# A fixed tile per expert for its last rows, and eight dense groups ahead of the expert stage

## The chip, the core and the metric

The kernel runs on one core of a Trainium2 chip, all in fp32. The metric is the device time of one execution in microseconds; times here are the median of three runs, and the profile is of one execution.

## What is computed

For x of 16 x 512 tokens of width 256, with xn = layernorm(x), the output is x + attn(xn) + ffn(xn):

```python
# attn: a diagonal state space model, then a gated FFN (D_FF = 688)
u = rmsnorm(xn, ssm_norm_w);  Bu = u @ B_w.T                  # 64 states
h_t = sigmoid(log_lambda) * h_(t-1) + Bu_t                    # along 512 tokens
x1 = xn + h @ C_w.T + D_skip * u;  z = rmsnorm(x1, ffn_norm_w)
attn = x1 + (silu(z @ w1.T) * (z @ w3.T)) @ w2.T
# ffn: 32 experts of inner width 128, 8 per token, and one shared expert (256)
scores = sigmoid(xn @ gate_w.T)       # top 8 within the 4 best groups of 4, normalised, times 2.5
ffn = sum_e combine[t, e] * (silu(xn @ w_gate[e].T) * (xn @ w_up[e].T)) @ w_down[e].T + shared(xn)
```

## The kernel before

The 8192 tokens are 64 tiles of 128 and 16 groups of four tiles (a group is one sequence of 512). Each of five engines runs its own instruction list, ordered by hand; semaphores tie them together.

**Stages.** First (a0) all groups are loaded, normalised and sent through the router. Then come the early dense groups 0 to 8 (FIRST = 9), then the expert stage, then the late dense groups 9 to 15.

**A dense group** (`pe_group`, `act_group`, `dve_group`) has eight steps s. Step s computes a gate and an up product (line 1263; steps 0 and 1 are the shared expert and read xT, the others read zT), ScalarE applies silu (648), VectorE multiplies (`h_tile`, 991), and TensorE adds the down product of the step before (1280). Between the steps stands the preparation of the next group: transposing its xn (step 1), B product (2), scan (3), C product and x1 (4), norm (5, 6), transposing z at the end. `finish_part` adds what the group gives to x + x1; SP stores early groups' sums in DRAM (`parts`).

**Routing** is VectorE's work, done in halves of 32 tiles within the early groups: choice of experts in groups 0 and 1 to 3, slots and bases at the end of groups 0 and 3 (`r_slots`, `r_bases`, 823 to 852), the slot table and the weights between steps 0 and 1 of groups 1 and 4 (`r_slot_table`, `r_weights`, 857 to 875), the experts of the tiles one step later (`r_tile_experts`).

**Slots.** In each half the rows of tokens are sorted by expert in DRAM (`sorted_rows`), 288 tiles of 128 rows for 256 tiles' worth of rows. An expert with n rows has ceil(n / 128) tiles. Those that form pairs come first, so that the first SAME = 128 of 144 pairs hold one expert; each odd last tile goes behind. Rows of a last tile that no token fills must be zero: tiles from 224 on are zeroed at fixed addresses, and one further 128-row store of zeros per expert goes to an address that `r_bases` computes (`pad_starts`): for half 0, 16 by SP and 16 by GpSimd (537), for half 1, 32 by SP (407). Then GpSimd scatters rows with their routing weights, one indirect DMA per tile and choice, 256 per half (546).

**Expert stage.** 288 pairs of tiles. Per pair: load rows, transpose (1336), gate and up products (`e_gu`, 1348: four matmul calls over 256 columns for one expert, eight over 128 for two; the trace has two matmuls per call), silu (680), product (1108), down product (1362), scaling (690, 1117), store to `results`. VectorE copies each pair's gate and up weights to a fixed place (1100): one block for one expert, two for two. Expert weights (`wexp`, 12.6 MB) lie in `big`, where the routing scratch, the x buffers (from AT_X) and the rows of half 0 (from AT_ROWS) were before; so SP loads them in parts as each gets free, the last ones behind the scatter of half 0 (420). GpSimd gathers each token's eight results (557), for half 0 within the pairs of half 1, for half 1 in the late stage; VectorE sums them (1009, 1016): half 0's within the pairs of half 1, half 1's (`combine`) in the late groups, four tiles in each, and the last four at the very end.

**Borders.** Into the experts: VectorE and ScalarE wait until all early sums are stored, TensorE for row loads and weights. Out of them, group 9 is prepared by itself:

```python
            transpose_x(FIRST)          # TensorE, after e_down(ALL - 1)
            bu_product(FIRST)
            bu_transpose(FIRST)
            y_product(FIRST)
            transpose_z(FIRST)
```

## Time and profile before

| | |
|---|---|
| median of three runs | 1827.65 us (1825.58 to 1830.5) |
| the profiled execution | 1828.46 us, its span 1826.8 us |
| granted TensorE clock, mean | 0.969 of 2.4 GHz |
| TensorE / VectorE / ScalarE / GpSimd busy | 1732.0 / 986.1 / 653.4 / 1042.6 us |
| early groups from, expert stage, late groups from | 88.6, 556.7 to 1459.9, 1489.3 us |

Times in rows are us from the span's start, unless they are called ns. PE is TensorE, PEld its weight loads, DVE VectorE, ACT ScalarE, POOL GpSimd, SP the engine that issues most DMAs. In a timeline "x8" stands for eight instructions put together, and the bracket is the idle time before them and what ended it. The clock column is the granted share of 2.4 GHz.

### The profile page before, as it was taken

Reading aid. Unit: us, or ns where it says so; the run is one execution under the profiler, and the core shown is the slowest. Engines: PE = TensorE matmul, PEld = TensorE weight load, DVE = VectorE, ACT = ScalarE, POOL = GpSimd, SP = SyncE. Lnnn points to the kernel's source line nnn. Section 1 sums busy time; section 2 is a strip of 40 time slices with the busy share of each in tenths; the row PEclk is TensorE's granted clock in tenths of the full one; section 3 lists DMA queues with packets and bytes.
Section 4 is the critical chain, followed back from the end, with each engine's and each line's share of the span. In section 5 each row is a group of like instructions: output and inputs, shape, how many; then the busy total and the mean of one; then the engine's idle time right before and its main releaser. Section 6 shows DMA issues by size and latency. Waiting matters only on the chain.

```text
span 1826.8 us, 26818 instructions
## 1 busy us (share of the span) xinstructions
PE 1732.0 (95%) x7846; PEld 1259.9 (69%) x7848; DVE 986.1 (54%) x2832; ACT 653.4 (36%) x1349; POOL 1042.6 (57%) x1058
## 2 busy tenths in 40 slices
PE   7797899899998999999999999999999969999996
PEld 3464565566666888888889888888888846666663
DVE  7487646633313444444445566666666535555555
ACT  6520221222213444444444444444444422222220
POOL 0002777777777777773000566666656077777773
PEclk9798999899998999999999999999999969999998
DMA  5964333636378999997555899999899554443332
GB/s 171 323 224 139 134 140 115 223 128 252 126 277 274 297 292 300 293 296 248 180 176 179 255 295 274 287 276 288 275 284 277 175 158 123 123 121 110 110 110 75
DMA packets 270790, 383.71 MB, mean 210 GB/s; under 512 B 30916, under 2 KB 235832, under 8 KB 269880
## 3 DMA queue, kind: packets, MB, share of 16 engines
q1 hardware_dynamic: 220584, 236.94, 41.1%
q0 software_dynamic: 49920, 145.03, 24.1%
q8 instruction: 66, 1.08, 0.2%
q14 instruction: 76, 0.62, 0.1%
q10 hardware_dynamic: 144, 0.03, 0.0%
HBM read 189.47 MB, written 192.42 MB: 209 GB/s over the span
## 4 chain that ended last, share of the span: by engine, by line
PE 89%; DVE 7%; issue 1%; ACT 1%; DMA 1%; DVEq 0%; SPq 0%; ACTq 0%
PE ps L1348 29%; PE ps L1263 19%; PE ps L1362 14%; PE ps L1280 11%; PE ps L1336 7%; PE ps L1183 2%; PE ps L1245 2%; PE ps L1216 2%; PE ps L1255 1%; PE ps L1232 1%; PE ps L1176 1%; DVE big L1009 1%; DMA big<-in_x 0%; PE ps L1239 0%; DVE arena L991 0%
## 5 line engine op out<-in xcount | busy, mean ns | idle before, releaser
L557 POOL DMA_INDIRECT xe<-results,slots x384 | 391.9, 1020 | 395.8 <-DMA results<-arena 217.4
L1348 PE MATMUL ps<-arena 128*128 128x256 f32 (+1 forms) x2560 | 573.5, 369 | 1.5 <-ACT arena L675 1.5
L1348 PEld LDWEIGHTS ps<-arena 128*128 128x128 f32 x2560 | 428.6, 190 | 106.1 <-ACT arena L675 66.0
L1100 DVE COPY arena<-big 128x512 f32 x320 | 138.7, 442 | 345.4 <-PE ps L1348 318.6
L546 POOL DMA_INDIRECT sorted_rows<-big,slots x256 | 260.5, 1017 | 84.0 <-issue 77.8
L1362 PE MATMUL ps<-big,arena 128*128 x1152 | 296.4, 380 | 0.3 <-DVE arena L1108 0.3
L546 POOL DMA_INDIRECT sorted_rows<-xe,slots x256 | 248.3, 970 | 78.1 <-issue 78.1
L1263 PE MATMUL ps<-arena,w 128*128 128x512 f32 x640 | 288.4, 593 | 0.0
L648 ACT ACTIVATE arena<-ps 128x512 f32<-128x512 f32 (+1 forms) x128 | 76.4, 597 | 559.4 <-PE ps L1263 515.5
L991 DVE TENSOR_TENSOR arena<-arena,ps 128x512 f32<-128x512 f32 (+1 forms) x128 | 88.0, 688 | 329.3 <-ACT arena L648 328.2
L680 ACT ACTIVATE arena<-ps 128x256 f32<-128x256 f32 x288 | 110.6, 384 | 377.0 <-PE ps L1348 377.0
L1362 PEld LDWEIGHTS ps<-big,arena 128*128 128x128 f32 x1152 | 196.4, 190 | 15.4 <-issue 0.7
L1263 PEld LDWEIGHTS ps<-arena,w 128*128 128x128 f32 x640 | 122.2, 191 | 119.5 <-issue 115.2
L1280 PE MATMUL ps<-w,arena 128*128 128x256 f32 (+1 forms) x768 | 186.3, 385 | 1.7 <-DVE arena L991 1.7
L675 ACT ACTIVATE arena<-ps 128x512 f32<-128x512 f32 x288 | 172.1, 597 | 26.1 <-PE ps L1336 11.0
L1336 PE MATMUL ps<-ident,arena 128*128 128x128 f32 x1152 | 173.8, 274 | 6.4 <-DMA arena<-sorted_rows 6.4
L1280 PEld LDWEIGHTS ps<-w,arena 128*128 128x128 f32 (+1 forms) x768 | 142.8, 191 | 50.7 <-issue 31.1
L1117 DVE TENSOR_SCALAR arena<-ps,wcol 128x256 f32<-128x256 f32 x288 | 139.0, 483 | 68.1 <-PE ps L1362 60.4
L690 ACT ACTIVATE arena<-ps,wcol 128x256 f32<-128x256 f32 x288 | 136.6, 474 | 92.6 <-PE ps L1362 91.0
L1336 PEld LDWEIGHTS ps<-ident,arena 128*128 128x128 f32 x1152 | 143.5, 141 | 32.8 <-issue 6.9
L557 POOL DMA_INDIRECT big<-results,slots x128 | 130.4, 1019 | 39.0 <-issue 39.0
L1263 PE MATMUL ps<-arena,shgu 128*128 128x512 f32 x256 | 123.4, 638 | 7.1 <-DVEq L819 7.1
(186 smaller groups left out, 1402.8 us busy)
## 6 DMA issues: line engine op xcount, KB each, us to landing
arena<-sorted_rows SPq DMA_DIRECT2D x288, 288.0 KB
results<-arena SPq DMA_DIRECT2D x288, 256.0 KB, 3.6
sorted_rows<-big SPq DMA_DIRECT2D x2, 9216.0 KB, 47.3
big<-in_x SPq DMA_DIRECT2D x32, 512.0 KB, 4.5
sorted_rows<-big SPq DMA_DIRECT2D x48, 144.0 KB, 1.9
xe<-results,slots POOLq DMA_INDIRECT x384, 4.0
out<-xe SPq DMA_DIRECT2D x48, 128.0 KB, 3.9
big<-in_wexp SPq DMA_DIRECT2D x1, 5632.0 KB, 19.3
```

Source lines behind the costliest of these rows:

```text
L546: pool.indirect_dma_start(out=sorted_rows[half], out_offset=bass.IndirectOffsetOnAxis(ap=slots[:, half * HT + t, k:k + 1], axis=0), in_=ro ...
L557: pool.indirect_dma_start(out=gathered_at[place(i)][:, k, :], out_offset=None, in_=results[half], in_offset=bass.IndirectOffsetOnAxis(ap=s ...
L675: nc.scalar.activation(rT[n % 2], ps[:, n % 2, :], ACT.Copy).then_inc(rT_ready, 1)
L680: nc.scalar.activation(eg[n % 2], ps[:, 2 + n % 2, 0:2 * P].rearrange("p (s i) -> p s i", s=2), ACT.Silu).then_inc(eg_ready, 1)
L690: nc.scalar.activation(ey[n % RING][:, 0, :], ps[:, 4 + 2 * (n % 2), 0:D], ACT.Copy, scale=wcol[:, n % RING, 0:1]).then_inc(ey_act, 1)
L1100: last = nc.vector.tensor_copy(wgu[n % 2][:, s, :], big[:, ds(at_w, 4 * INNER)])
L1117: tsc(ey[n % RING][:, 1, :], ps[:, 5 + 2 * (n % 2), 0:D], wcol[:, n % RING, 1:2], None, ALU.mult).then_inc(ey_dve, 1)
L1263: last = mm(ps[:, 2 + 2 * (s % 2) + u, :], w[:, u, c, lo:lo + P], src[:, c, :], start=c == 0, stop=c == DC - 1)
L1280: last = mm(ps[:, 6 + t // 2, (t % 2) * D:(t % 2 + 1) * D], h[c % HR][at_p, t * P:(t + 1) * P], w, start=False, stop=s == CH - 1 and t % 2 ...
L1336: last = tp(ps[:, n % 2, j * P:(j + 1) * P], rows[n % RING][:, s, c * P:(c + 1) * P], ident[:, :])
L1348: last = mm(ps[:, 2 + n % 2, (2 * u + s) * P:(2 * u + end) * P], wgu[n % 2][:, s, at_w:at_w + INNER], rT[n % 2][:, (2 * c + s) * P:(2 * c ...
L1362: last = mm(ps[:, 4 + 2 * (n % 2) + s, 0:D], eh[n % 2][:, s, :], big[:, ds(at_w + 2 * D, D)], start=True, stop=True)
```

## The change

An expert with n rows now has floor(n / 128) full tiles, in pairs first as before and then singly, and always one more tile, number 256 + e of the half, for the rest. Tiles from 224 on are zeroed at fixed addresses as before; all of `store_padding` goes, on SP and on GpSimd. The full tiles can fill fewer pairs surely: SAME is 96 in place of 128. The sorted rows have 288 tiles in each half as before, and so the stage 288 pairs.

FIRST is 8. Group 8 is still prepared within group 7, but its products come first of the late stage. Its xT, zT and its sum x + x1 are kept in DRAM meanwhile and loaded again near the end of the expert stage. The scatter is counted in eighths, and the weights over the rows of half 0 are loaded in eight parts.

```diff
-    SAME = HT * K // 2
-    USED = 2 * SAME - E
-    SPAN = NSLOT + E * P
+    FULL_TILES = HT * K
+    SAME = FULL_TILES // 2 - E
+    USED = FULL_TILES - E
+    SPAN = NSLOT
...
-    FIRST = 9
+    FIRST = HT // GT
     LATE = range(FIRST, GROUPS)
-    QUARTER = HT // 4
+    PIECES = 8
+    PIECE = HT // PIECES
...
-            def store_padding(half, es):
-                sp.wait_ge(starts_ready, half + 1)
-                sp.wait_ge(padded[half], 16)
-                for e in es:
-                    start = sp.value_load(pad_starts[half][0:1, e:e + 1], min_val=0, max_val=SPAN - P)
-                    sp.dma_start(sorted_rows[half][ds(start, P), :], pad_row).then_inc(padded[half], 16)
...
-            store_padding(0, range(E // 2))
             for g in range(FIRST - 1):
-                if g + 4 < FIRST:
+                if g + 4 <= FIRST:
...
-            sp.wait_ge(x_used, FIRST)
-            load_wexp(AT_X, AT_ROWS)
-            sp.wait_ge(xposed, FIRST)
-            for j in range(4):
-                sp.wait_ge(scattered[0][j], 16 * K * QUARTER)
-                load_wexp(AT_ROWS + j * QUARTER * ROW, AT_ROWS + (j + 1) * QUARTER * ROW)
-            store_part(FIRST - 1)
...
-            sp.wait_ge(zposed, FIRST)
-            sp.wait_ge(gu_ready, CH * (FIRST - 1) + 2)
-            sp.wait_ge(rms_z_ready, FIRST)
+            def load_wexp_over_rows(j):
+
+                sp.wait_ge(scattered[0][j], 16 * K * PIECE)
+                load_wexp(AT_ROWS + j * PIECE * ROW, AT_ROWS + (j + 1) * PIECE * ROW)
+
+            sp.wait_ge(x_used, FIRST)
+            sp.wait_ge(xposed, FIRST)
+            for j in range(PIECES - 1):
+                load_wexp_over_rows(j)
+            sp.wait_ge(xT_ready, FIRST + 1)
+            sp.dma_start(kept_xT, xT.rearrange("p c n -> p (c n)")).then_inc(xT_stored, 16)
+            sp.wait_ge(x_used, FIRST + 1)
+            load_wexp(AT_X, AT_ROWS)
+            sp.dma_start(group_rows(parts, FIRST), part_early[FIRST % 2]).then_inc(part_kept, 16)
+            sp.wait_ge(xT_stored, 16)
+            sp.wait_ge(y_ready, FIRST + 1)
+            sp.wait_ge(z_ready, FIRST + 1)
+            scattered_all(sp, 0)
             for n in range(RING):
                 load_rows(n)
+            load_wexp_over_rows(PIECES - 1)
+            sp.wait_ge(zT_ready, FIRST + 1)
+            sp.dma_start(kept_zT, zT.rearrange("p c n -> p (c n)")).then_inc(zT_stored, 16)
+            store_part(FIRST - 1)
...
+                    if m == ALL - 3:
+                        sp.dma_start(xT.rearrange("p c n -> p (c n)"), kept_xT).then_inc(xT_reloaded, 16)
...
-            sp.wait_ge(wgu_ready, ALL)
-            for g in range(FIRST, FIRST + 4):
+            for q in range(2):
+                sp.wait_ge(ey_stored[q], 16 * (ALL // RING))
+            sp.wait_ge(zT_stored, 16)
+            sp.dma_start(zT.rearrange("p c n -> p (c n)"), kept_zT).then_inc(zT_reloaded, 16)
+            for g in range(FIRST + 1, FIRST + 5):
                 load_x(g, g)
-            for i in range(HT, HT + GT):
-                load_part(i)
+            sp.wait_ge(part_kept, 16)
+            sp.dma_start(part_of(FIRST), group_rows(parts, FIRST)).then_inc(part_reloaded, 16)
             for g in LATE:
                 for t in range(GT):
-                    store_out((g - 1) * GT + t)
-                    if t == 2 and g + 4 < GROUPS:
-                        sp.wait_ge(x_used, g + 1)
-                        load_x(g + 4, g + 4)
+                    if g > FIRST:
+                        store_out((g - 1) * GT + t)
+                    if t == 2 and g + 5 < GROUPS:
+                        sp.wait_ge(x_used, g + 2)
+                        load_x(g + 5, g + 5)
...
-            pool.wait_ge(starts_ready, 1)
-            pool.wait_ge(padded[0], 16)
-            for e in range(E // 2, E):
-                start = pool.value_load(pad_starts[0][0:1, e:e + 1], min_val=0, max_val=SPAN - P)
-                pool.dma_start(sorted_rows[0][ds(start, P), :], pad_row).then_inc(padded_by_pool, 16)
-            pool.wait_ge(padded_by_pool, 16 * (E // 2))
-            pool.wait_ge(padded[0], 16 * (E // 2 + 1))
             for half in range(HALVES):
-                if half:
-                    pool.wait_ge(padded[1], 16 * (E + 1))
+                pool.wait_ge(padded[half], 16)
...
-            act.wait_ge(ey_dve, ALL)
-            xT_copy(FIRST)
-            results_stored(act, ALL)
-            rms_z(FIRST)
-            zT_copy(FIRST)
...
-            def r_bases(half):
-
-                tsc(nt_u, ne, float(P - 1), None, ALU.add)
+            def r_bases():
+
                 do(nc.vector.tensor_copy(full_u, ne))
-                tsc(nt_u, nt_u, P.bit_length() - 1, None, ALU.logical_shift_right)
                 do(tsc(full_u, full_u, P.bit_length() - 1, None, ALU.logical_shift_right))
                 nc.vector.memset(ones_e, 1.0)
-                nc.vector.tensor_copy(unused_f, unused_u)
+                nc.vector.tensor_copy(part_at, part_u)
                 nc.vector.tensor_copy(full, full_u)
-                tsc(two_u, nt_u, 1, None, ALU.logical_shift_right)
-                do(nc.vector.tensor_copy(ntf, nt_u))
+                do(tsc(two_u, full_u, 1, None, ALU.logical_shift_right))
                 do(nc.vector.tensor_copy(two, two_u))
-                tt(in_part, ntf, full, ALU.subtract)
                 do(tsc(two, two, 2.0, None, ALU.mult))
-                tt(odd, ntf, two, ALU.subtract)
+                tt(odd, full, two, ALU.subtract)
+                tsc(cut_part, full, float(P), None, ALU.mult)
                 do(nc.vector.tensor_tensor_scan(endt, ones_e, two, 0.0, ALU.mult, ALU.add))
                 do(nc.vector.tensor_tensor_scan(end_odd, ones_e, odd, 0.0, ALU.mult, ALU.add))
-                tsc(first_odd, endt[:, E - 1:E], float(2 * SAME), None, ALU.max)
                 tt(base, endt, two, ALU.subtract)
-                do(tsc(cut, two, float(P), None, ALU.mult))
+                tsc(cut, two, float(P), None, ALU.mult)
                 do(tsc(end_odd, end_odd, first_odd, None, ALU.add))
+                tt(apart_part, part_at, end_odd, ALU.subtract)
                 do(tt(apart, end_odd, odd, ALU.subtract))
-                tt(full, full, base, ALU.add)
                 do(tt(apart, apart, endt, ALU.subtract))
-                do(tt(odd, odd, apart, ALU.mult))
-                do(tt(full, full, odd, ALU.add))
-                do(tt(full, full, unused_f, ALU.subtract))
-                do(tt(full, full, in_part, ALU.mult))
                 tsc(base, base, float(P), 1.0, ALU.mult, ALU.add)
-                tsc(apart, apart, float(P), None, ALU.mult)
-                do(tt(full, full, unused_f, ALU.add))
-                tsc(pad_starts[half], full, float(P), None, ALU.mult).then_inc(starts_ready, 1)
+                tsc(apart_part, apart_part, float(P), None, ALU.mult)
+                do(tsc(apart, apart, float(P), None, ALU.mult))
             def r_slot_table(half):
-                by_expert, past = (a.rearrange("p (e t) -> p e t", t=HT) for a in (work, wt))
-                do(tt(past, by_expert, cut.unsqueeze(2).to_broadcast([P, E, HT]), ALU.is_ge))
-                do(tt(past, past, apart.unsqueeze(2).to_broadcast([P, E, HT]), ALU.mult))
+                by_expert, past, past_full = (a.rearrange("p (e t) -> p e t", t=HT) for a in (work, wt, table))
+                tt(past, by_expert, cut.unsqueeze(2).to_broadcast([P, E, HT]), ALU.is_ge)
+                do(tt(past_full, by_expert, cut_part.unsqueeze(2).to_broadcast([P, E, HT]), ALU.is_ge))
+                tt(past, past, apart.unsqueeze(2).to_broadcast([P, E, HT]), ALU.mult)
+                do(tt(past_full, past_full, apart_part.unsqueeze(2).to_broadcast([P, E, HT]), ALU.mult))
+                do(tt(wt, wt, table, ALU.add))
...
+                tsc(te_part, tile_f, float(FULL_TILES), None, ALU.is_ge)
+                tsc(tile_f, tile_f, -float(FULL_TILES), None, ALU.add)
...
+                do(tsc(tile_f, tile_f, float(E - 1), None, ALU.min))
+                do(tt(tile_f, tile_f, te_f, ALU.subtract))
+                do(tt(tile_f, tile_f, te_part, ALU.mult))
+                do(tt(te_f, te_f, tile_f, ALU.add))
...
-                    elif s % 2 == 1:
+                    elif s % 2 == 1 and g > FIRST:
...
-                dve_group(g, g + 1 < FIRST)
+                dve_group(g, True)
...
-            dve.wait_ge(ey_act, ALL)
-            a1_norm(FIRST)
-            bu_scale(FIRST)
-            scan(FIRST)
-            make_x1(FIRST)
-            make_z(FIRST)
...
+                        if g == FIRST:
+                            pe.wait_ge(zT_reloaded, 16)
...
-            transpose_x(FIRST)
-            bu_product(FIRST)
-            bu_transpose(FIRST)
-            y_product(FIRST)
-            transpose_z(FIRST)
+            pe.wait_ge(xT_reloaded, 16)
             pe.wait_ge(ey_act, ALL)
             pe.wait_ge(ey_dve, ALL)
```

## Rows read from the trace of the kernel before

**Rows 1.** the page, parts 1 and 5: busy us, share or mean ns

```profile
PE 1732.0 (95%) x7846; PEld 1259.9 (69%) x7848; DVE 986.1 (54%) x2832; ACT 653.4 (36%) x1349; POOL 1042.6 (57%) x1058
...
L1100 DVE COPY arena<-big 128x512 f32 x320 | 138.7, 442 | 345.4 <-PE ps L1348 318.6
```

**Rows 2.** chain that ended last, in order of time: start us, us

```profile
508.13 7.06 PE ps L1263 x16
...
562.04 1.99 PE ps L1348 x8
958.20 1.87 PE ps L1348 x16
...
1408.09 1.87 PE ps L1348 x16
...
1452.55 1.87 PE ps L1348 x16
...
1537.83 7.06 PE ps L1263 x16
...
1770.21 7.06 PE ps L1263 x16
```

**Rows 3.** stretches: us, busy of PE PEld DVE ACT POOL, clock, DMA, GB/s

```profile
508.00:548.50 40.50, 40.50 (x127) 23.52 (x126) 6.79 (x10) 4.77 (x8) 30.73 (x33) 1.00 0.77 298
548.50:562.00 13.50, 5.74 (x17) 4.13 (x16) 3.05 (x10) 1.58 (x3) 10.14 (x12) 0.62 0.79 262
...
1460.00:1489.50 29.50, 12.43 (x45) 10.03 (x46) 11.75 (x24) 4.78 (x13) 20.14 (x20) 0.55 0.61 190
```

**Rows 4.** timeline at the border out of the experts: start us, us, instruction

```profile
1458.73 1.12 PE L1362 MATMUL ps<-big,arena 128*128 x4 [0.27 <-DVE arena L1108]
...
1460.93 2.18 SPq L369 DMA_DIRECT2D big<-in_x  x4
...
1465.95 1.50 DVE L738 TENSOR_SCALAR big<-big,rstd,nmr 128x256 f32<-128x256 f32 x4 [5.52 <-DMA big<-in_x]
...
1489.32 9.10 PE L1263 MATMUL ps<-arena,shgu 128*128 128x512 f32 x16
```

**Rows 5.** timeline of VectorE in the routing of half 0

```profile
147.83 0.18 DVE L823 TENSOR_SCALAR big<-big 128x32 uint32<-128x32 f32 x1
...
152.66 0.68 DVE L991 TENSOR_TENSOR arena<-arena,ps 128x512 f32<-128x512 f32 x1
153.26 1.22 DVE L857 TENSOR_TENSOR big<-big 128x1024 f32<-128x1024 f32 x1
...
168.31 0.69 DVE L991 TENSOR_TENSOR arena<-arena,ps 128x512 f32<-128x512 f32 x1 [0.22 <-DVE big L875]
```

**Rows 6.** TensorE's waits for the gate product: sum us, times, longest us

```profile
PE ps L1280 <- DVE arena L991: 15.3, 4, 7.1
```

**Rows 7.** timeline of GpSimd: first scatter of half 0, first of half 1

```profile
181.18 1.04 POOL L546 DMA_INDIRECT sorted_rows<-big,slots  x1 [6.24 <-DMA sorted_rows<-big]
...
519.74 0.96 POOL L546 DMA_INDIRECT sorted_rows<-xe,slots  x1 [0.30 <-issue]
```

**Rows 8.** timeline at the border into the experts

```profile
549.92 0.38 SPq L424 DMA_DIRECT2D parts<-arena  x1
...
554.99 0.76 DVE L1100 COPY arena<-big 128x512 f32 x2 [5.15 <-issue]
...
556.72 3.78 PE L1348 MATMUL ps<-arena 128*128 128x256 f32 x8 [0.77 <-ACT arena L675]
```

**Rows 9.** landings of weight loads, then of half 0's scatters

```profile
DMA to landing us min/median/max: 7.9/14.8/20.3
...
DMA to landing us min/median/max: 2.4/2.5/16.5
```

**Rows 10.** SP's own waits

```profile
SPq L420 <- DMA sorted_rows<-big,slots: 16.4, 1, 16.4
```

**Rows 11.** timeline of GpSimd: the last gather

```profile
1801.96 0.95 POOL L557 DMA_INDIRECT big<-results,slots  x1 [0.30 <-issue]
```

More of the change, by code:

```diff
@@ L168, in build @@
         top_slots = scratch(HT * K)
-        ne, ntf, endt, base, nt_f, ones_e, full_f, full, unused_f, unused_i = (scratch(E) for _ in range(10))
-        two_f, two, odd, end_odd, apart, cut, first_odd, te_odd, te_late = (logits[:, k * E:(k + 1) * E] for k in range(9))
+        ne, endt, base, ones_e, full_f, full, part_at, part_i = (scratch(E) for _ in range(8))
+        two_f, two, odd, end_odd, apart, cut, apart_part, cut_part, te_odd, te_late, te_part = (
+            logits[:, k * E:(k + 1) * E] for k in range(11))
         two_u = two_f.bitcast(U32)
-        first_odd, te_odd, te_late = first_odd[:, 0:1], te_odd[:, 0:TE_C], te_late[:, 0:TE_C]
-        nt_u, full_u, unused_u = nt_f.bitcast(U32), full_f.bitcast(U32), unused_i.bitcast(U32)
-        in_part = nt_f
+        first_odd = endt[:, E - 1:E]
+        te_odd, te_late, te_part = te_odd[:, 0:TE_C], te_late[:, 0:TE_C], te_part[:, 0:TE_C]
+        full_u, part_u = full_f.bitcast(U32), part_i.bitcast(U32)
         den = scratch(HT)
@@ L181, in build @@
         pad_row = scratch(ROW)
-        pad_starts = [scratch(E).bitcast(U32) for _ in range(HALVES)]
         ssmw_row = wt[:, 0:D]
@@ L288, in build @@
         part_stored = sems("part_stored", 2)
-        scattered = [sems(f"scattered{h_}_", 4) for h_ in range(HALVES)]
+        scattered = [sems(f"scattered{h_}_", PIECES) for h_ in range(HALVES)]
         wexp_loaded = sem("wexp_loaded")
@@ L304, in build @@
         gathered = sems("gathered", DEEP)
+        xT_stored = sem("xT_stored")
+        zT_stored = sem("zT_stored")
+        part_kept = sem("part_kept")
+        xT_reloaded = sem("xT_reloaded")
+        zT_reloaded = sem("zT_reloaded")
+        part_reloaded = sem("part_reloaded")
         part_loaded = sems("part_loaded", RING)
@@ L359, in scattered_all @@
         def scattered_all(eng, half):
-            for j in range(4):
-                eng.wait_ge(scattered[half][j], 16 * K * QUARTER)
+            for j in range(PIECES):
+                eng.wait_ge(scattered[half][j], 16 * K * PIECE)
         @block.sync
@@ L433, in _ @@
                     turn_tile_experts(0)
-                if g == 3:
-                    store_padding(1, range(E))
                 if g == 4:
@@ L439, in _ @@
                     sp.wait_ge(routing_done, 2)
-                    sp.wait_ge(padded[0], 16 * (E // 2 + 1))
-                    sp.wait_ge(padded_by_pool, 16 * (E // 2))
-                    sp.wait_ge(padded[1], 16 * (E + 1))
+                    for half in range(HALVES):
+                        sp.wait_ge(padded[half], 16)
                     load_wexp(0, AT_X)
-            sp.wait_ge(x_used, FIRST)
-            load_wexp(AT_X, AT_ROWS)
-            sp.wait_ge(xposed, FIRST)
-            for j in range(4):
-                sp.wait_ge(scattered[0][j], 16 * K * QUARTER)
-                load_wexp(AT_ROWS + j * QUARTER * ROW, AT_ROWS + (j + 1) * QUARTER * ROW)
-            store_part(FIRST - 1)
             def load_rows(n):
@@ L527, in _ @@
             nc.gpsimd.iota(tile_u, pattern=[[1, TE_C]], base=0, channel_multiplier=TE_C)
-            nc.gpsimd.iota(unused_u, pattern=[[1, E]], base=NTILE, channel_multiplier=0)
+            nc.gpsimd.iota(part_u, pattern=[[1, E]], base=FULL_TILES, channel_multiplier=0)
             step.wait()
@@ L548, in _ @@
                             out_offset=bass.IndirectOffsetOnAxis(ap=slots[:, half * HT + t, k:k + 1], axis=0),
-                            in_=rows_of[half][:, t, :], in_offset=None).then_inc(scattered[half][t // QUARTER], 16)
+                            in_=rows_of[half][:, t, :], in_offset=None).then_inc(scattered[half][t // PIECE], 16)
             scattered_all(pool, 1)
@@ L687, in e_out @@
                 act.wait_ge(ey_ready, n + 1)
+                if n == 0:
+                    act.wait_ge(zT_stored, 16)
                 if n >= RING:
@@ L935, in route_late @@
                     r_slots(half, 1)
-                    r_bases(half)
+                    r_bases()
             def a1_norm(g):
-                if g in LATE:
+                if g > FIRST:
                     dve.wait_ge(x_loaded[g % 4], 16 * ((GROUPS + g) // 4 + 1))
@@ L1114, in e_out @@
                 dve.wait_ge(ey_ready, n + 1)
+                if n == 0:
+                    dve.wait_ge(zT_stored, 16)
                 if n >= RING:
```

24 lines of the change are left out of this document (13 added, 11 removed).

## The prediction

> **What bounds the kernel now.** I read the page first. TensorE is busy 95% of the span [rows 1], so only what TensorE waits for, or does at its lower clock, can be won. Next I read the chain that ended last, to find stage borders: dense groups up to 548.5 us, expert pairs from 556.7 to 1459.9 us, dense groups again to the end. In the late stage a dense group costs (1770.21 - 1537.83) / 5 = 46.48 us [rows 2]. Then the table by stretches: group 8, the last early one, whose stretch holds no preparation of a next group, runs 40.5 us without a gap; the border into the experts has TensorE busy 5.74 of 13.5 us at granted clock 0.62, the border out of them 12.43 of 29.5 us at 0.55 [rows 3]. These borders, and two waits for VectorE's routing work (7 us each, one per half), are nearly all the idle time there is after 125 us. The borders and the routing were then read in order of time.
>
> **The change, part by part.** Everything is counted on the profiled execution: span 1826.8 us, 1828.46 us as a time.
>
> *Group 9's preparation standing alone.* Now the last expert matmul ends at 1458.73 + 1.12 = 1459.85 us, and the first dense product of group 9 starts at 1489.32 us [rows 4]: 29.5 us for loading x, transposing, the recurrence, the norm and transposing again, one after the other. Group 9 then takes until 1537.8 us, 48.4 us, because it begins at the lower clock: 2.0 us over the 46.48 of its successors. The change prepares group 8 inside group 7 as before, keeps it in DRAM, and reads it back; the first late group needs no preparation on its own. Gone: 31.5 us.
>
> In its place come two small waits. TensorE waits until ScalarE and VectorE have emptied the last pair, about 0.75 us. Then products 0 and 1 of group 8 need only xT, asked for three pairs ahead. The next step, transposing group 9's x, waits for its load: SP asks for it now at 1460.93, and VectorE can normalise at 1465.95 [rows 4]. SP must now first issue zT's reload, so I put the normalised tile at 1461.5 + 5.0 + 1.5 = 1468.0 us against the two products' end, 1460.6 + 7.06 = 1467.7 (sixteen such matmuls take 7.06 us [rows 2]). VectorE's first gate product stands behind this normalisation and comes just after it. With a half-megabyte transfer ahead in the queue I allow 1.2 us (0 to 3). Added: 2.0 us. Every late group still waits its turn in the same order.
>
> *Group 9's preparation, interleaved.* It moves into group 8, which was 40.5 us without a preparation [rows 3] and becomes a 46.48 us group: +6.0 us.
>
> *More pairs with two experts.* Of 144 pairs per half, 128 now share one expert; afterwards 96 do. So 64 pairs change from eight 256-column matmuls to sixteen 128-column ones, and VectorE copies two weight blocks for them. The trace has 32 such pairs. A one-expert pair takes (958.20 - 562.04) / 127 = 3.119 us, a mixed one (1452.55 - 1408.09) / 14 = 3.176 us, and the latter are the pairs of half 1 that share VectorE with the sums [rows 2]. 64 x 0.057 = +3.6 us. From below, nothing; from above, the whole second copy, 0.442 us [rows 1], on the path: 28.3 us. I take the rows of the same operation.
>
> *Routing.* The base computation takes 152.66 - 147.83 = 4.8 us for 30 small operations [rows 5]; 12 go and 3 come, and of 16 that wait for their predecessor 11 stay. At 0.23 us for such and 0.09 us for the others that is 3.4 us: -1.5. The slot table gets three more 128x1024 operations of 1.22 us plus gap [rows 5]: +3.7. So the second gate product of group 1 (168.31 us now) comes 2.2 us later. TensorE waits for exactly that product, 7.1 us, the longest of four such waits that sum to 15.3 us [rows 6]; half 1's is most of the rest, 6.6 us. Added: 2 x 2.2 = 4.4 us. The tile tables' six further small operations (1.0 us) delay only the third gate product, which is needed 5 us later: nothing. Bounds 0 (were the wait hidden) to 2 x 3.2.
>
> *Padding.* The 64 stores with data-dependent addresses (48 by SP, 16 by POOL) go. None is on the chain; what they hold up is the scatter. It starts at 181.18 us and its 256th issue ends at 519.5 [rows 7], 338 us long; routing is ready just ahead of VectorE's next gate product at 168.31 [rows 5], at 168.1 us. Afterwards it starts at about 168.1 + 2.2 + 0.4 = 170.7 us and, with a few delayed issues fewer, ends near 507 us. That is what makes an expert start one group earlier possible: the eighth group would end TensorE's work at 508.1 [rows 2] + 4.4 = 512.5 us.
>
> *The border into the experts.* Now TensorE ends at 548.5 and the first pair begins at 556.72: 8.2 us, of which SP's store of the last partial sums (549.92) until VectorE may copy weights (554.99) is 5.1 [rows 3, 8]. Afterwards SP waits for the scatter (about 510 us with its landing), then issues four row loads, the last eighth of the weights, the copy of zT and the store of group 7's sums, in that order; VectorE's and ScalarE's first expert work waits behind the last of these, and TensorE behind them. That is 1.15 + 0.59 + 0.52 + 0.52 = 2.8 MB from 510 us on; the table has 298 GB/s for this core's transfers between 508 and 548 us [rows 3], so 9.3 us, and 2 us to land: VectorE starts at about 521.5, and the first pair 1.7 us later as now, near 523.2. That is 10.7 us after TensorE's end instead of 8.2: +2.5 us. From below 0 (the present 5.1 us after the store); from above the longest landing that a weight load shows, 20.3 us against its shortest 7.9 [rows 9]: +12 more.
>
> How much a busy queue holds back the scatter decides here. SP waited 16.4 us for the scatter of half 0 [rows 10], until 529.1 us when it issued the last weight load, 9.6 us after POOL had issued the last scatter; scatters landed in 2.5 us at the median and 16.5 at the longest [rows 9]. Those 5.5 MB of weight loads and stores were queued at 510 us. Afterwards seven of the eight pieces are asked for once 7/8 of the scatter is through, near 470 us, and 4.1 MB at 298 GB/s are in by 486; 2.5 MB more are asked for some 13 us before group 7 ends, near 500 us, and are in by 509: hence my 510.
>
> The Trainium skill, "DMA: Bandwidth & Descriptors", section "Queues, rings and completion order", says that each DMA engine takes turns between queues packet by packet. By that rule a scatter would not wait out the other queue's backlog, and the border would stay at 8.2 us, the sum 2.5 us lower. The 9.6 us here speak for the longer wait, so I keep it.
>
> *The end.* Gathers of half 1 start when the expert pairs' results are stored and issue the last at 1801.96 us [rows 11], 25 us before the span's end. The late stage gets 17 us longer (a group of 46.48 us more, 29.5 less), the gathers start at the same place in it, so their cover grows: no term.
>
> **The sum.** -31.5 + 2.0 + 6.0 + 3.6 + 4.4 + 2.5 = -13.0 us: 1828.46 - 13.0 = 1815.5. The profiled execution is 0.8 us above the median of the three runs, 1827.65. I say 1815 us.
>
> **Rivals.** *A, the sum as above.* 1815, its own range 1808 to 1821. Chance 0.60.
>
> *B, the expert start is held by transfers.* The row loads or the last weights land late, as the slowest weight load did; TensorE then idles 23 us at this border and falls to its lower clock as it does now [rows 3]. For it: SP issues five dependent things after the scatter, in one queue. Against it: most weights are in by then. 1815 + 12 = 1827, no change. Chance 0.16.
>
> *C, the small costs vanish.* The border stays at 8.2 us, and the routing's 4.4 us are absorbed by what follows. Against it: TensorE is seen waiting for that very product. 1815 - 2.5 - 4.4 = 1808. Chance 0.14.
>
> *D, slower: two-expert pairs are not cheap in long rows.* 48 of them in a row per half, instead of 16, make the second weight copy the bound: 1815 - 3.6 + 28.3 = 1840. From 0.26 us per pair ((13.0 + 3.6) / 64) on, the kernel is slower than before. For it: VectorE also does half 1's sums, and it copies, scales and multiplies in every step. Against it: 14 steps beside the sums all keep 3.176 us [rows 2]. Chance 0.06.
>
> The Trainium skill, "TensorE: Matmul & The Clock Gate", section "LDWEIGHTS (loading the stationary operand)", puts a load at its columns over 1.2 GHz, 107 ns for 128. An estimate from that page: eight loads more in 64 pairs, if none were hidden, 55 us, so 1866. The trace disagrees, as a mixed pair costs 0.057 us more.
>
> The remaining 0.04 is for what I haven't seen.
>
> **How the numbers follow.** Times within 0.3% (5.5 us) can't be told from no change. Faster takes A, C and the low edge of B: 0.77. Same is most of B and the high edge of A: 0.14. Slower is D and the rest: 0.09. The range of 8 in 10 runs from a little under C to the lower half of B: 1805 to 1825.
>
> **What would show it.** Right: between the last expert matmul and the first dense product under 2 us instead of 29.5; mixed pairs at 3.17 to 3.18 us in both halves, 48 in a row; the first pair near 523 us; the first scatter near 171 us; waits of about 9 us for VectorE near 171 and 337 us; groups of 46.5 us, eight late. Wrong: a first pair after 535 us (B), pairs of over 3.4 us (D), or late groups longer than 46.5 us because gathers or the reloads run late.

## The result and the profile after

| | median us | runs | profiled execution, its span |
|---|---|---|---|
| before | 1827.82 | 8 (1825.58 to 1830.5) | 1828.46, 1826.8 |
| after | 1823.03 | 8 (1819.34 to 1824.54) | 1819.34, 1817.6 |
| after, run again with the experiments | 1820.61 | 5 (1819.13 to 1823.78), before beside it 1827.25 | span 1820.7 |

The ratio is 0.997 (0.9959 to 0.998), and 0.9966 (0.9953 to 0.9979) the second time: faster by 5 to 7 us where 13 were forecast, at the edge of what can be told from no change. The profiled execution of after is the fastest of its eight, so each step is read from two executions of the same kernel, the second one 3.1 us longer and, at 1822.48 us, near the first median.

| us against before, from the spans' parts | forecast | after | after again |
|---|---|---|---|
| end of the eighth group (before: start of group 8's products, 508.13 [rows 2]) | +4.4 | +6.9 | +6.6 |
| TensorE's end to the first expert pair | +2.5 | +4.8 | +5.5 |
| expert stage | +3.6 | +3.0 | +5.7 |
| group 8 moved, group 9's preparation | -23.5 | -23.9 | -23.9 |
| sum | -13.0 | -9.2 | -6.1 |

The largest term is right. The routing and the border into the experts, and in the second execution the expert stage too, ate the rest. The page, parts 1 and 4 (busy us and share; shares of the chain):

```profile
PE 1728.4 (95%) x8358; PEld 1277.1 (70%) x8360; DVE 1009.1 (56%) x2896; ACT 652.5 (36%) x1349; POOL 1031.5 (57%) x1042
PE 74%; POOL 14%; issue 5%; DVE 4%; DMA 1%; ACT 1%; SPq 0%; DVEq 0%; POOLq 0%
```

TensorE is as busy as before [rows 1]; new is that 14% of the chain runs over GpSimd, whose scatter of half 0 now sets the start of the experts. The chain's pieces (start us, us, what):

```profile
508.82 4.72 DMA sorted_rows<-big,slots
516.67 9.45 DMA parts<-arena
527.96 3.63 PE ps L1351 x8
829.08 1.87 PE ps L1351 x16
...
978.30 1.87 PE ps L1351 x16
...
1482.12 7.06 PE ps L1264 x16
...
1760.98 7.06 PE ps L1264 x16
```

The last scatter is issued at 508.82 and takes 4.72 us to land; the store of group 7's sums, last of seven transfers that SP issues then, takes 9.45 us, where [rows 8] had 5.1 between that store's issue and VectorE's first copy. The 47 pairs between 829.08 and 978.30 take 3.175 us each, and late groups (1760.98 - 1482.12) / 6 = 46.48, both as forecast. The timeline of this border:

```profile
513.63 1.95 SPq L443 DMA_DIRECT2D arena<-sorted_rows  x4
...
515.62 0.53 SPq L422 DMA_DIRECT2D big<-in_wexp  x1
516.19 0.43 SPq L477 DMA_DIRECT2D kept_zT<-arena  x1
516.67 0.50 SPq L426 DMA_DIRECT2D parts<-arena  x1
526.28 0.60 ACT L681 ACTIVATE arena<-ps 128x512 f32<-128x512 f32 x1 [12.10 <-DMA parts<-arena]
527.38 0.76 DVE L1105 COPY arena<-big 128x512 f32 x2 [11.08 <-issue]
```

TensorE's last dense matmul ends at 514.98. Row loads, weights, zT and sums, 2.8 MB, are issued from 513.63 to 517.17, while GpSimd goes on with half 1's scatter; ScalarE and VectorE stand until the sums have landed. The stretches of this border, of after and then of the second execution (columns as in [rows 3]):

```profile
515.00:528.00 13.00, 0.67 (x5) 0.49 (x5) 1.90 (x4) 0.60 (x1) 9.81 (x11) 0.60 0.93 328
528.00:534.00 6.00, 5.32 (x18) 4.21 (x19) 1.15 (x7) 0.98 (x2) 4.78 (x5) 0.72 0.53 162
534.00:540.00 6.00, 6.00 (x33) 4.97 (x32) 2.72 (x10) 2.91 (x6) 4.48 (x6) 1.00 0.81 260
```

```profile
528.00:534.00 6.00, 4.88 (x13) 3.69 (x14) 1.73 (x8) 0.98 (x2) 4.48 (x6) 0.50 0.47 161
534.00:540.00 6.00, 6.00 (x21) 4.80 (x22) 1.43 (x5) 1.46 (x3) 4.70 (x5) 0.67 0.61 182
```

The DMA engines are 93% busy in those 13 us, at 328 GB/s: the wait is for transfers. Then the clock: TensorE has stood idle but for four transposes. In 528 to 534 the second execution is granted 0.50, the lower level of 1.2 GHz, and 0.67 in 534 to 540; the first 0.72 and then the full 2.4 GHz. The second execution's second pair takes 5.18 us instead of 3.14. That is 2.0 us, most of what the two differ by. The border out of the experts:

```profile
1432.99 1.13 PE L1365 MATMUL ps<-big,arena 128*128 x4 [0.26 <-DVE arena L1113]
1434.95 7.11 PE L1264 MATMUL ps<-arena,shgu 128*128 128x512 f32 x16 [0.83 <-DVE arena L1124]
1435.24 0.41 SPq L506 DMA_DIRECT2D arena<-kept_zT  x1
1435.70 2.21 SPq L378 DMA_DIRECT2D big<-in_x  x4
1440.96 1.41 DVE L741 TENSOR_SCALAR big<-big,rstd,nmr 128x256 f32<-128x256 f32 x4 [6.27 <-DMA big<-in_x]
```

0.83 us instead of 29.5 [rows 4], at full clock; x is normalised 8.3 us after the last expert matmul, where 8.2 were forecast. VectorE's routing in group 1 and TensorE's waits for it:

```profile
152.21 1.22 DVE L851 TENSOR_TENSOR big<-big 128x1024 f32<-128x1024 f32 x1
...
170.82 0.69 DVE L994 TENSOR_TENSOR arena<-arena,ps 128x512 f32<-128x512 f32 x1 [0.22 <-DVE big L872]
```

```profile
PE ps L1281 <- DVE arena L994: 19.9, 4, 9.1
PE ps L1351 <- DVE arena L1105: 10.7, 1, 10.7
```

From the slot table's first operation to the gate product it is 18.6 us, 15.05 before [rows 5]: +3.56, forecast +3.7. The waits grow from 15.3 [rows 6] to 19.9 us, +4.6, forecast +4.4. The eighth group ends 6.9 us later all the same: the dense groups start 0.35 us later (88.75 for 88.40), the waits make 4.6, and the remaining 1.9 come outside these waits. For the second wait the stretches behind it show where, before and then after, each from the end of its wait (334.87 and 341.31 us):

```profile
334.90:342.00 7.10, 7.10 (x15) 4.45 (x16) 3.20 (x14) 0.00 (x0) 5.43 (x6) 0.66 0.69 244
342.00:349.00 7.00, 7.00 (x26) 4.09 (x25) 1.85 (x3) 1.20 (x2) 5.17 (x7) 1.00 0.65 228
```

```profile
341.30:348.40 7.10, 7.09 (x14) 4.44 (x15) 3.96 (x21) 0.00 (x0) 5.40 (x6) 0.60 0.32 123
348.40:355.40 7.00, 7.00 (x25) 3.90 (x24) 1.81 (x2) 0.82 (x2) 5.19 (x6) 1.00 0.29 108
```

A wait of 6.6 us is followed by 7.1 us at 0.66, one of 9.1 us by 7.1 us at 0.60, and both by the full clock. That is worth 0.4 us up to the end of group 7. The other 1.4 to 1.5 us lie between the two waits, where the clock is lower than before too: 0.91 for 0.93 in the 26 us behind the first wait, and 0.56 for 0.66 in the 10 us behind a wait of 3.9 us (it ends at 208.61, before at 205.48) that is no longer than before. Why the clock is lower there isn't shown.

### The profile page after: what moved, and what is told of

It reads as the page before. It is cut to its first block, busy times and chain, and to the rows that moved or that the text cites. A ratio compares the mean times of both kernels' runs of the same rounds, so it can differ in the third digit from the quotient of the medians.

```text
span 1817.6 us, 27587 instructions
## 1 busy us (share of the span) xinstructions
PE 1728.4 (95%) x8358; PEld 1277.1 (70%) x8360; DVE 1009.1 (56%) x2896; ACT 652.5 (36%) x1349; POOL 1031.5 (57%) x1042
## 3 DMA queue, kind: packets, MB, share of 16 engines
q8 instruction: 70, 1.15, 0.3%
## 4 chain that ended last, share of the span: by engine, by line
PE 74%; POOL 14%; issue 5%; DVE 4%; DMA 1%; ACT 1%; SPq 0%; DVEq 0%; POOLq 0%
PE ps L1351 29%; POOL sorted_rows L552 14%; PE ps L1365 14%; PE ps L1264 11%; PE ps L1339 7%; PE ps L1281 6%; PE ps L1184 2%; PE ps L1177 1%; PE ps L1217 1%; PE ps L1246 1%; PE ps L1233 1%; PE ps L1256 1%; DMA big<-in_x 1%; DMA parts<-arena 1%; DVE big L1014 1%
## 5 line engine op out<-in xcount | busy, mean ns | idle before, releaser
L563 POOL DMA_INDIRECT xe<-results,slots x384 | 388.0, 1010 | 379.9 <-DMA results<-arena 198.6
L1351 PE MATMUL ps<-arena 128*128 128x256 f32 (+1 forms) x3072 | 577.2, 336 | 11.4 <-DVE arena L1105 10.7
L1351 PEld LDWEIGHTS ps<-arena 128*128 128x128 f32 x3072 | 456.4, 191 | 105.0 <-ACT arena L681 64.4
L1105 DVE COPY arena<-big 128x512 f32 x384 | 160.0, 438 | 351.1 <-PE ps L1351 326.4
L1365 PEld LDWEIGHTS ps<-big,arena 128*128 128x128 f32 x1152 | 196.7, 191 | 15.3 <-issue 0.7
```

The source lines that it names most:

```text
L563: pool.indirect_dma_start(out=gathered_at[place(i)][:, k, :], out_offset=None, in_=results[half], in_offset=bass.IndirectOffsetOnAxis(ap=s ...
L1105: last = nc.vector.tensor_copy(wgu[n % 2][:, s, :], big[:, ds(at_w, 4 * INNER)])
L1351: last = mm(ps[:, 2 + n % 2, (2 * u + s) * P:(2 * u + end) * P], wgu[n % 2][:, s, at_w:at_w + INNER], rT[n % 2][:, (2 * c + s) * P:(2 * c ...
L1365: last = mm(ps[:, 4 + 2 * (n % 2) + s, 0:D], eh[n % 2][:, s, :], big[:, ds(at_w + 2 * D, D)], start=True, stop=True)
```

## The experiments

All were timed beside the kernel before, on three chips: the first four rows of the table with before at 1827.25 us, the next four at 1827.07, the last three at 1827.17. Rows of different chips are compared by their ratios. In the table, "rows" is SP's first row load, "pair" TensorE's first expert matmul, "border" the time from TensorE's last dense matmul to that pair (us, one profiled execution each).

| kernel | median us | ratio to before (95%) | rows | pair | border |
|---|---|---|---|---|---|
| after again | 1820.61 | 0.9966 (0.9953 to 0.9979) | 513.29 | 528.43 | 13.7 |
| no wait for sums | 1818.15 | 0.9951 (0.9939 to 0.9963) | 515.47 | 527.11 | 10.3 |
| layout alone | 1840.49 | 1.0073 (1.006 to 1.0086) | 557.88 | 563.79 | 7.8 |
| eight groups alone | 1822.66 | 0.9981 (0.9972 to 0.999) | 519.42 | 534.31 | 26.4 |
| weights early | 1814.42 | 0.9933 (0.992 to 0.9946) | 513.30 | 520.82 | 6.0 |
| scatter held | 1819.68 | 0.9956 (0.9944 to 0.9969) | 515.30 | 528.56 | 12.0 |
| routing split | 1820.41 | 0.9961 (0.9949 to 0.9974) | 514.77 | 529.34 | 17.3 |
| all pairs mixed | 1833.56 | 1.0032 (1.0023 to 1.0041) | 514.77 | 529.83 | 13.8 |
| eight groups, border mended | 1816.83 | 0.9947 (0.9934 to 0.9961) | 519.90 | 527.71 | 20.6 |
| weights early, scatter held | 1813.55 | 0.9926 (0.9913 to 0.994) | 514.08 | 521.57 | 6.2 |
| the same, routing split | 1811.43 | 0.9919 (0.9905 to 0.9932) | 510.05 | 517.30 | 8.7 |

**The change once more**, as it is, beside the others.

> The changed kernel once more, for a second trace of it. The profiled execution was the fastest of eight, 3.7 us under their median, and its trace accounts for 9.2 us of gain where the median shows 4.8. Theory: executions differ at the border into the experts, where transfers that land late hold back all engines; a slower execution shows the first expert pair later than 527.96 us by as much as its time is longer, and the expert stage (906.2 us) and the late stage (383.5 us) as before. Rival: they differ in the granted clock after the two routing waits, then the end of group 7 (514.98 us) moves. Second rival: the expert stage itself is longer. Median 1821 to 1825 us.

It gave 1820.61 us, and the second column of the table of steps. The theory misses: of the 3.1 us by which this execution is longer, the first pair shows 0.5 (528.43 for 527.96), the end of group 7 is 0.3 earlier, the late stage is the same, and 2.7 are the expert stage (908.8 for 906.2 us), which is the second rival.

**No wait for the sums.** Of the two buffers of early sums only the first is reused by the experts; group 7's store need not be waited for.

```diff
-            for par in range(2):
-                act.wait_ge(part_stored[par], 16 * len(range(par, FIRST, 2)))
+            act.wait_ge(part_stored[0], 16 * (FIRST // 2))
```

(VectorE the same, and it waits for the store of group 8's sums besides; SP's wait moves into pair 8.)

> VectorE and ScalarE no longer wait, ahead of their first expert work, for the store of group 7's sums (its buffer is not reused in the expert stage); SP asks for it eight pairs later. Theory: this store, 9.5 us on its way behind 1.15 MB of rows, 0.6 MB of weights and 0.5 MB of zT, sets the start of the experts; without it the last piece of weights does, landing near 521.5 us, so the first pair moves from 527.96 to about 522.5 us and the time falls by 5 us, to 1818 us. Rival: the last weights land as late as that store, since all share the same engines; then the first pair stays after 526 us and the gain is under 1.5 us.

ScalarE starts at once, and the last piece of the weights takes the store's place (timeline of this kernel, then pieces of its chain):

```profile
517.48 0.56 SPq L422 DMA_DIRECT2D big<-in_wexp  x1
...
519.55 0.60 ACT L682 ACTIVATE arena<-ps 128x512 f32<-128x512 f32 x1 [3.58 <-PE ps L1339]
526.35 0.94 DVE L1105 COPY arena<-big 128x512 f32 x2 [8.27 <-issue]
```

```profile
517.48 6.88 DMA big<-in_wexp
...
524.44 1.17 DVEq L1096
...
525.63 0.58 DVEq L1097
```

From the first row load to the first pair it is 11.6 us instead of 14.3 (after) and 15.1 (after again). Half a confirmation: the sums did hold the start, but the weights stood right behind them. They landed at 524.36 us where 521.5 was expected, and the first pair came at 527.11, after 526 as the rival said; 1818.15 us is the time that the theory named, but the interval overlaps that of the change, so by time alone no gain is shown. The chain also shows a piece that no sum has: between the landing and the first copy VectorE reads its tables of experts (lines 1096 and 1097), 2.0 us here and 1.2 in after. This reading needs neither rows nor weights; no run puts it ahead of the wait.

**Layout alone**: nine early groups, the new slots.

```diff
-    SAME = HT * K // 2
+    SAME = FULL_TILES // 2 - E
...
     FIRST = 9
```

> The new slot layout alone, with the dense groups as before the change (nine early, group 9 prepared by itself). Theory: it costs 6.5 us by the longer waits for the routing and the lower clock after them (4.4 us were forecast) and 3.0 to 3.6 us by 64 more two-expert pairs, and the earlier scatter gains nothing, since group 8 covers it: 1828 + 10 = 1838 us. Rival 1: only the terms as forecast, 1828 + 8 = 1836 us. Rival 2: without the 64 stores something else gets faster, 1828 us or less.

It costs 13.2 us by the medians, where 4.4 + 3.6 were forecast by the prediction and 10 expected here. In the profile the early stage ends 7.5 us later (555.99, before 548.52), and the expert stage is 5.6 us longer: 3.7 for mixed pairs and 1.9 for a second pair at the lower clock (5.01 us).

**Eight groups alone**: the change with the old slots and their zero stores.

```diff
-    SAME = FULL_TILES // 2 - E
+    SAME = HT * K // 2
...
     FIRST = HT // GT
```

> Eight early groups with the old layout and its stores of zeros. The scatter then starts near 181 and ends near 519.5 us, group 7 ends near 508 us. Theory: the experts start when the scatter has landed and the rows and the last weights after it, near 530 us (26 us earlier than before the change), pairs cost what they did, and the late stage is 16.5 us longer: 1828 - 10 = 1818 us, so faster than the whole change. Rival: the scatter's landing behind the weight loads costs more (as 9.6 us before the change), first pair after 537 us, 1825 us or more: then the layout is what makes the change pay.

4.6 us faster than before beside it by the medians (1827.25), where the whole change gave 6.6 on the same chip. TensorE is done at 507.91 us, 7 earlier than in after, and then waits 14.6 us for rows, since the scatter starts later (180.83 us). The first pair comes at 534.31 us, 4 later than expected, and the time is 1822.66 where 1818 was. SP's wait for the scatter, and the border:

```profile
SPq L372 <- DMA sorted_rows<-big,slots: 16.5, 1, 16.5
```

```profile
519.42 2.00 SPq L455 DMA_DIRECT2D arena<-sorted_rows  x4
...
534.31 3.32 PE L1371 MATMUL ps<-arena 128*128 128x256 f32 x7 [10.74 <-DVE arena L1125]
```

Rows to pair again take 14.9 us. So the layout brings the first pair 5.9 to 6.4 us earlier, through the scatter's earlier end, and pays 3.7 us of that in pairs; the intervals of the two ratios overlap, so by time its worth isn't shown at this border.

**Weights early**: no wait for the sums, and the last piece of the weights goes second.

```diff
-            for n in range(RING):
-                load_rows(n)
-            load_wexp_over_rows(PIECES - 1)
+            load_rows(0)
+            load_wexp_over_rows(PIECES - 1)
+            for n in range(1, RING):
+                load_rows(n)
```

> As the run without the wait for group 7's sums, and SP asks for the last piece of weights after one pair's rows in place of four. Theory: the experts start when the last weights have landed, and that is a matter of the bytes ahead of them at this border; 0.3 MB of rows ahead in place of 1.15 MB bring the first pair from 11.6 us after SP's first row load to about 8, so to 521 to 523 us, and the time falls by 3 to 4 us more, to 1814 or 1815 us. Rival: the weights' landing is a matter of latency or of all that is queued, also behind them; then the first pair stays at 11 us after the row load and the time at 1818 us.

The same transfers in another order:

```profile
513.30 0.38 SPq L443 DMA_DIRECT2D arena<-sorted_rows  x1
513.73 0.49 SPq L422 DMA_DIRECT2D big<-in_wexp  x1
514.27 1.53 SPq L443 DMA_DIRECT2D arena<-sorted_rows  x3
...
520.25 0.97 DVE L1106 COPY arena<-big 128x512 f32 x2 [4.14 <-issue]
520.82 3.69 PE L1352 MATMUL ps<-arena 128*128 128x256 f32 x8 [3.77 <-DVE arena L1106]
```

7.5 us from rows to pair instead of 14.3 to 15.1, a border of 6.0 us, and 1814.42 us. That the total now is the forecast's is luck: this border is 2.2 us shorter than before the change, where the forecast had it 2.5 us longer, and that pays for the routing, 6.7 us here as in after. How much of the gain is the order's and how much the dropped wait's isn't settled, as the interval overlaps that of the run that only drops the wait.

**Scatter held**: GpSimd starts half 1's scatter after the weights are in.

```diff
+                if half:
+                    pool.wait_ge(wexp_loaded, 16 * WEXP_LOADS)
```

> The changed kernel; GpSimd holds the scatter of half 1 until all expert weights are loaded. Theory: at the border the DMA engines are full, and the scatter of half 1, 116 GB/s of their traffic, is what stretches 2.8 MB to 13 us; without it the first pair comes 10 to 11 us after the first row load in place of 14.3 to 15.1, time 1817 to 1819 us; half 1's scatter ends 15 us later, near 850 us, and isn't missed before 970 us. Rival: the small packets of the scatter take no share that matters, gain under 1 us.

Rows to pair 13.3 us, only 1.1 to 1.9 less, where 3 to 5 were expected: the scatter's share of the border is small, and the store of the sums still ends it (ScalarE's 10.91 us). From SP's first row load to the landing of the sums it is 11.3 us, where it was 12.5 and 13.4 with the scatter beside them. The time is within the noise of the change's:

```profile
524.67 0.96 POOL L554 DMA_INDIRECT sorted_rows<-xe,slots  x1 [13.26 <-DMA big<-in_wexp]
526.72 0.60 ACT L683 ACTIVATE arena<-ps 128x512 f32<-128x512 f32 x1 [10.91 <-DMA parts<-arena]
```

**Routing split**: slot table, weights and tile experts at steps 0, 1 and 2 instead of 0, 0 and 1.

```diff
                     if g == after and s == 0:
                         r_slot_table(half)
+                    if g == after and s == 1:
                         r_weights(half)
-                    if g == after and s == 1:
+                    if g == after and s == 2:
                         r_tile_experts(half)
```

> The changed kernel; the second gate product of groups 1 and 4 stands between slot table and weights, the third before the tile tables, so that TensorE waits about 4 us there in place of 9 in each half. Theory: the early groups end 10 to 13 us earlier (near 503 us), but the experts' start hangs on the scatter, which starts 0.7 us later; the first pair stays near 528 us and the time between 1820 and 1824 us. Rival: TensorE's own work sets the start, then it falls by 8 us or more.

TensorE's waits in this kernel (us in total, times, longest):

```profile
PE ps L1282 <- DVE arena L995: 11.1, 4, 5.1
PE ps L1241 <- DVE arena L952: 5.8, 5, 2.3
```

8.8 us less for the gate product, 3.7 more for the recurrence (line 952, 2.1 before the split); the eighth group ends only 2.6 to 2.9 us earlier, at 512.09, which misses the 10 to 13 expected. The first pair doesn't move, 529.34, nor does the time. That fits: the scatter and the transfers behind it set the start, not TensorE. The last scatter was issued at 512.27 us here, 3.5 later than in after, and landed in 2.4 us instead of 4.7.

**All pairs mixed**: no pair is taken for one expert's.

```diff
-    SAME = FULL_TILES // 2 - E
+    SAME = 0
```

> The changed kernel with all 288 pairs treated as two-expert pairs, 192 more than now. Theory: each costs 0.057 us more, 192 x 0.057 = 11 us, 1833 us, and every pair takes 3.175 us in both halves. Rival D of the prediction: in long rows the second weight copy of 0.44 us comes onto the path, in half 1 at least: 40 us or more on top.

192 more pairs cost 919.70 - 908.83 = 10.9 us of expert stage, 0.057 each. The chain's pieces in half 0:

```profile
699.21 1.88 PE ps L1351 x16
...
1137.39 1.88 PE ps L1351 x16
```

(1137.39 - 699.21) / 138 = 3.175 us with all in a row; over both halves the mean of the 285 steps behind the two slow ones is 3.175 too, and the time is 1833.56 us for 1833 expected. Rival D falls.

**Eight groups, border mended**: the old slots with weights early and no wait for sums.

> Eight early groups with the old layout, and the border put right as in the run with the weights first. Theory: the start of the experts is the scatter's landing plus the transfers behind it; the scatter lands 6 us later with the old layout, so the first pair comes near 527 us in place of 520.8, and the pairs cost 3 us less: 1814.4 + 6.2 - 3.0 = 1817.6 us; what the layout is worth in itself is then 3 us. Rival: TensorE's longer idle time costs clock as well, 1820 us or more.

1816.83 against 1814.42 us with the new slots, and a first pair at 527.71, both as expected. The medians, each against its own runs of before, say that the layout is worth 2.3 us once the border is right; the intervals of the ratios overlap, so its sign isn't settled by time. In the profile it moves the first pair from 527.71 to 520.82 and pays 3.7 us in pairs.

**Weights early and scatter held**, then **the same with the routing split**.

> The border put right (no wait for group 7's sums, last weights behind one pair's rows) and the scatter of half 1 held until the weights are in. Theory: with 0.9 MB ahead the scatter's share is worth 1 us or less at the start, and the later rows and stores come sooner: 1813 to 1814.5 us. Rival: holding the scatter costs as much as it gives, 1815 us or more.

> The same with the routing's gate products drawn apart (second one between slot table and weights). Theory: the early groups end 3 to 4 us earlier, but the scatter starts 0.7 us later and sets the start of the experts: 0 to +1 us against the run before it, 1813 to 1815.5 us. Rival: TensorE's earlier end shows, 1811 us or less.

1813.55 and 1811.43 us, the latter the fastest kernel here, 0.9919 (0.9905 to 0.9932) of before and faster than the change. Its border:

```profile
508.69 1.28 DVE L1005 TENSOR_TENSOR arena<-arena,ps 128x512 f32<-128x512 f32 x2 [3.21 <-PE ps L1285]
510.05 0.38 SPq L443 DMA_DIRECT2D arena<-sorted_rows  x1
510.48 0.46 SPq L422 DMA_DIRECT2D big<-in_wexp  x1
...
516.73 0.89 DVE L1109 COPY arena<-big 128x512 f32 x2 [6.76 <-issue]
```

The last scatter in the run without the split, then in this one (start of its issue, us to its landing):

```profile
509.19 4.81 DMA sorted_rows<-big,slots
```

```profile
507.55 2.42 DMA sorted_rows<-big,slots
```

Here the split came with a first pair at 517.30 instead of 521.57, where I had expected no gain: group 7 ends 6.7 us earlier (508.65), the last scatter is issued 1.6 us earlier, and it lands 2.4 us sooner. The landing goes with the split. SP asks for 2 MB of weights and for the store of group 8's 0.5 MB of sums as soon as the x buffers are free, within group 7. In the seven runs with eight groups, the new slots and no split, this comes 7.4 us ahead of the last scatter, which lands in 4.58 to 4.81 us; in the two with the split it comes 12.5 and 13.8 us ahead, in the two with the old slots 22.6 and 23.9, and in these four the scatter lands in 2.41 to 2.43 us. No run moves that request by itself, so this is a reading of the traces and not a test. The earlier issue isn't explained: in the split alone it was later. The first two pairs, at the lower clock, then take 2.6 us back (expert stage 908.8 against 906.3). The intervals of the two ratios overlap, so the 2.1 us between the medians aren't shown to be the split's. That holding the scatter adds to weights early (1813.55 against 1814.42) isn't shown either.

## Why the prediction missed

**The border into the experts failed.** The prediction put the first pair 10.7 us after TensorE's end instead of 8.2, a term of +2.5 us. It measured 13.0 and 13.7 us: +4.8 and +5.5. The 8.2 us were no good start for the sum: before, the chain runs over the first row load (issued at 550.41, landed after 4.32 us) and not over the store of the sums. Two steps of the working were off, in after about equally.

The first is the scatter's landing. The prediction had 2.5 MB of weights and sums asked for near 500 us "in by 509", and so the rows readable at 510, 2.5 us ahead of TensorE's end. They were asked for at 501.38; the weights landed after 8.8 us, at 510.2. The last scatter, issued at 508.82 (all 256 take 338 us as before, where a little less was expected), landed beside this traffic in 4.7 us (in 2.4 in the runs where this traffic was over), and SP's first row load came at 513.63, only 1.35 us ahead of TensorE's end: 1.15 us of the miss, and 1.1 in the second execution.

The second is the division of 2.8 MB by 298 GB/s, 11.5 us with the landing. It took 12.5 and 13.4 us, as the 2.8 MB did not have the DMA engines to themselves: 328 GB/s were moved, half 1's scatter included. With that scatter held it took 11.3. This is 1.0 and 1.9 us of the miss. The 1.7 us from there to the first pair were right in size (1.8), though in after two thirds of them are VectorE's reading of tables.

That VectorE and ScalarE wait behind the last of the transfers (seven, where rival B counts five) stood in the prediction. What it didn't ask is whether they must: nothing of the experts reads the sums or writes over their buffer, and with that wait dropped and the needed piece issued second the way from rows to pair took 7.5 us instead of 14.3 to 15.1. This is the mechanism of rival B, the expert start held by transfers, at 2.3 and 3.0 of its 12 us.

**The expert stage: one term absent.** The 64 mixed pairs cost what was said (3.175 against 3.118 us, 3.7 us). After the longer border the second pair can run at the lower clock too, +2.0 us; before, only the first did (5.32 us). In after as profiled the first was only partly slow (4.75 us) and the second not, hence +3.0 and +5.7. No term stood for the clock after a border that the sum itself had made longer.

**The routing's term, 4.4 us, was too small by 2.2 to 2.5.** VectorE's added work was right (3.56 us for 3.7) and TensorE's waits too (4.6 for 4.4); what comes on top while TensorE works, with a lower clock behind its waits, was left out (1.9 us in after), and the profiled start of the dense groups is 0.35 us later. The layout alone shows the same size, 7.5 us.

**Right:** the border out of the experts (0.83 us for 0.75, x ready 8.3 us after the last matmul for 8.2), group 8 among the late ones and 46.48 us for its successors, -23.9 for -23.5 in all; the first scatter at 171.55 us for about 171, though the last one's issue ended at 509.8 for near 507. Rival C falls, as both small costs are there and larger; so does D.

**The two places of the Trainium skill.** By the Trainium skill, "DMA: Bandwidth & Descriptors", section "Queues, rings and completion order", a scatter wouldn't wait out the other queue's backlog and the border would stay at 8.2 us; it was 13.0 and 13.7. The traces don't settle the rule: counted from its issue the last scatter landed in 10.6 us before the change (5.5 MB queued), in 4.7 after it (2.6 MB, 7.4 us earlier) and in 2.4 where these came 12.5 us earlier or more, so the traffic does lengthen it, by turns or by waiting. The rest of the border lay in SP's own list of transfers, which that rule doesn't touch. By the Trainium skill, "TensorE: Matmul & The Clock Gate", section "LDWEIGHTS (loading the stationary operand)", eight more loads a pair would be an estimated 0.86 us if none were hidden; 192 pairs show 0.057.

## What to carry to other kernels

When a stage is made to start earlier, list what it still has to fetch at the new moment, in the order of the queue, and tie each engine's start only to the transfer that it reads: here dropping a needless wait and moving one of seven transfers forward was worth 6 us (ratios 0.9966 and 0.9933, intervals apart), half of the forecast gain. Divide bytes by bandwidth only after adding what other queues move in the same stretch. And new idle time before a TensorE stretch needs a second line in the sum, for the lower clock behind it: here up to 1.9 us behind the waits of the early groups, and none or 2.0 us behind the border.

## What the hardware showed that was not expected

- How long TensorE stays at the lower clock behind a border differs between executions of one kernel: the second pair took 3.14 us in one and 5.18 in the other, after 13.0 and 13.7 us. It isn't the border's length alone: one slow pair behind 6.0, 8.2 and 26.4 us, two behind 7.8, 8.7 and 20.6. What decides it stays open.
- A store of 512 KB landed in 3.3 us at the median of the run and in 9.45 us as the last of seven transfers at this border; which of them is last is the writer's choice.
- A scatter of 128 rows landed in 4.6 to 4.8 us where 2.6 MB of another queue had been asked for 7.4 us ahead of it, and in 2.4 us where that was 12.5 us or more.
- Idle time costs again after it has ended, but here not for long: behind the second half's routing wait, 6.6 us before and 9.1 after, the clock is 0.66 and 0.60 for 7.1 us, then full in both, and the longer wait costs 0.4 us more than itself.
